# Layer 1 of a graph network: dense weights turned by transfers through memory, key one-hots in PSUM

## The reference

```
def _weighted_mean_agg(ft, w, src, dst, n_nodes):
    m = ft[src] * w[:, None]
    msum = segment_sum(m, dst, n_nodes)
    wsum = segment_sum(w, dst, n_nodes)
    safe = where(wsum > 0, wsum, 1.0)
    return where((wsum > 0)[:, None], msum / safe[:, None], 0.0)
neigh1 = _weighted_mean_agg(feat, w, src, dst, n)
neigh2 = _weighted_mean_agg(feat, w, dst, src, n)
```

## Time and profile before

| | us |
|---|---|
| median of 3 runs (9472.91 to 9473.69) | 9473.14 |
| the profiled execution | 9470.78 |
| its span, first to last instruction | 9469.0 |
| the stage of the change within it, first cell to last reversed product | 140.7 to 2975 |

### The profile page before, as it was taken

How to read it: one execution, slowest core, us unless ns; L and a number is a source line. 1 busy time by engine, 2 the same in 40 slices (tenths; PEclk the granted TensorE clock), 3 DMA queues, 4 the chain that set the end, 5 groups by cost and what they waited for, 6 DMA issues and landing times. The chain is left out here.

```text
span 9469.0 us, 228933 instructions
## 1 busy us (share of the span) xinstructions
PE 8637.6 (91%) x58595; PEld 6939.6 (73%) x58596; DVE 5874.3 (62%) x12349; ACT 5795.2 (61%) x15455; POOL 5415.5 (57%) x5229
## 2 busy tenths in 40 slices
PE   5999999999998899999988888888885899999998
PEld 5999999999997677775656666666654666666666
DVE  7777777787876677762125555555554555555555
ACT  5888888888885544440016677677763555555555
POOL 5777777777773000000005777777771677777775
PEclk7999999999999999999999999999998999999999
DMA  3111111111111122225544444444430222222222
GB/s 129 45 44 44 44 44 44 45 44 44 44 44 48 69 109 115 115 95 191 191 140 142 118 118 118 118 118 118 118 112 33 77 73 73 73 73 73 73 73 69
DMA packets 463488, 819.24 MB, mean 87 GB/s; under 512 B 160570, under 2 KB 330610, under 8 KB 443634
## 3 DMA queue, kind: packets, MB, share of 16 engines
q0 software_dynamic: 193536, 455.41, 16.6%
q1 hardware_dynamic: 269810, 362.04, 11.0%
HBM read 668.94 MB, written 147.98 MB: 86 GB/s over the span
## 5 line engine op out<-in xcount | busy, mean ns | idle before, releaser
L1776 POOL DMA_INDIRECT x<-table,p_gidx x1632 | 1542.4, 945 | 2375.3 <-ACT p_gidx L1813 1968.7
L618 POOL DMA_INDIRECT g_G<-table,g_runs x1776 | 2146.9, 1209 | 549.0 <-issue 538.8
L2228 POOL DMA_INDIRECT c_G<-table,c_gidx x1632 | 1543.7, 946 | 505.2 <-issue 497.0
L757 PE MATMUL g_ps_cell<-g_kw,g_loh 128*128 128x98 f32 x9472 | 1224.4, 273 | 28.6 <-DVE g_kw L675 28.6
L757 PEld LDWEIGHTS g_ps_cell<-g_kw,g_loh 128*128 128x128 f32 x9472 | 1154.6, 193 | 28.8 <-DVE g_kw L675 28.8
L1866 PE MATMUL p_ps_sum<-x 128*96 128x256 f32 x3264 | 898.5, 399 | 232.1 <-DVE hid L1802 223.1
L768 PE MATMUL g_ps_rev<-g_hrow,g_AT 128*128 128x129 f32 x7252 | 1047.6, 281 | 66.0 <-ACT g_AT L734 66.0
L768 PEld LDWEIGHTS g_ps_rev<-g_hrow,g_AT 128*128 128x128 f32 x7252 | 903.9, 192 | 94.0 <-ACT g_AT L734 94.0
L1866 PEld LDWEIGHTS p_ps_sum<-x 128*96 128x96 f32 x3264 | 469.0, 163 | 647.0 <-ACT x L1831 272.5
L1802 DVE TENSOR_TENSOR hid<-hid,p_ps_sum 96x256 f32 x1632 | 677.1, 415 | 363.8 <-DVE hid L1802 360.5
L1338 ACT CAST a_A<-a_ps_cell 128x392 bf16<-128x392 f32 x1184 | 510.8, 492 | 541.8 <-PE a_ps_cell L1372 541.8
(11 more groups left out here) (345 smaller groups left out, 16644.2 us busy)
## 6 DMA issues: line engine op xcount, KB each, us to landing
adj_save<-a_A SPq DMA_DIRECT2D x74, 1568.0 KB, 5.1
a_A<-adj_save SPq DMA_DIRECT2D x74, 1568.0 KB, 6.5
c_ed<-in_edge_dram SPq DMA_DIRECT2D x1632, 25.0 KB
g_G<-table,g_runs POOLq DMA_INDIRECT x1776
p_lhs<-in_edge_dram SPq DMA_DIRECT2D x1632, 16.0 KB
x<-table,p_gidx POOLq DMA_INDIRECT x1632
c_G<-table,c_gidx POOLq DMA_INDIRECT x1632
table<-m_rows SPq DMA_DIRECT2D x17, 384.0 KB
```

The costliest lines, as they stand in the source:

```text
L618: g.indirect_dma_start(G[:, e % GR, q, 0:D], None, table, bass.IndirectOffsetOnAxis(ap=runs[:, n % 2, 0, RQ * e + q:RQ * e + q + 1], axis= ...
L757: last = pe.matmul(ps_cell[q % 2][:, r * KEYS:(r + 1) * KEYS], loh[:, b, cell, :], kw[:, b, cell, :], start=True, stop=True)
L1776: g.indirect_dma_start(G[:, H * b + q, :], None, table2, bass.IndirectOffsetOnAxis(ap=gidx[:, b, q:q + 1], axis=0)).then_inc(gathered[b], 16)
L2228: g.indirect_dma_start(G[:, H * b + q, :], None, table, bass.IndirectOffsetOnAxis(ap=gidx[:, b, q:q + 1], axis=0)).then_inc(gathered[b], 16)
```

## The change

- **The dense matrix is no longer turned on TensorE.** Cells are made the other way round, with `kw` as weights and `loh` as the moving side, so that keys lie on partitions: 98 partitions by 4 x 128 columns a half. ScalarE copies a half into `X`, a ring of 8 halves. SyncE stores it to `turn_save` in memory (two batches), and after each four halves a quarter of a batch can be loaded back into `AT`, now with slots on partitions (32 partitions of 49 x 128 numbers a load). `AT` holds two whole batches.
- `turn`, the copies to `AT`, `ps_turn`, and the semaphores between them are gone. `backward` reads `AT` and waits for the four loads of its batch. It stands 5 halves later (`LATE`), at halves 6 to 15 of the next batch and 0 to 5 of the one after.
- **The key one-hots** are made in two operations of 4 slots, in float32, into the two freed PSUM banks, and `kw` is made from there in two operations as well. `number` is float32 now. `koh` has a wait for `oh_ready` of the chunk before.
- In the stage before this, the slots are numbered in another order, to fit the partitions of the loads.

The diff, cut to its core:

```
@@ stage_gru_sums
-                A = sb("g_A", [P, 2, KEYS, HALF], F32, ctx)
-                AT = sb("g_AT", [P, 2, TG * P], F32, ctx)
-                koh = sb("g_koh", [P, 2, 2, KEYS, CQ], BF16, ctx)
+                X = sb("g_X", [P, XR, CQ * P], F32, ctx)
+                AT = sb("g_AT", [P, 2, BUCKETS * P], F32, ctx)
-                ps_turn = [ps(f"g_ps_turn{k}", ctx) for k in range(2)]
+                ps_koh = [ps(f"g_ps_koh{k}", ctx) for k in range(2)]
@@ sync
+                        def store(n, bb, q):
+                            sp.wait_ge(evacd, HALVES * n + q + 3)
+                            sp.dma_start(turn_save[bb, CQ * q:CQ * (q + 1), :, :].rearrange("c k l -> k c l"),
+                                         X[0:KEYS, q % XR, :].rearrange("k (c l) -> k c l", c=CQ)).then_inc(stored[q // QT_HALVES], 16)
+                        def load_turned(m, b, z):
+                            sp.wait_ge(stored[z], 16 * QT_HALVES * (m + 1))
+                            sp.dma_start(AT[QSLOTS * z:QSLOTS * (z + 1), b, :],
+                                         turn_save[b, HALF // QUARTERS * z:HALF // QUARTERS * (z + 1), :, :].rearrange("c (j h) l -> (c j) (h l)", j=GRP)
+                                         ).then_inc(turned[b], 16)
+                        def body(i, bb):
...
+                            for q in range(HALVES):
+                                if known(n):
+                                    store(n, bb, q)
+                                if q == 1 and known(n - 1):
+                                    load_turned(n - 1, 1 - bb, QUARTERS - 1)
+                                if known(n) and q == 9:
+                                    if known(n - 2):
+                                        sp.wait_ge(rev_made, TGS * (n - 1))
+                                    load_turned(n, bb, 0)
+                                    load_turned(n, bb, 1)
+                                if known(n) and q == 13:
+                                    load_turned(n, bb, 2)
@@ vector, one_hots
-                            v.tensor_tensor(koh[:, b % 2, :, :, :],
-                                            key_tab[:, cells].rearrange("p (u r) -> p u r", u=2).unsqueeze(2).to_broadcast([P, 2, KEYS, CQ]),
-                                            number[:, :, :].unsqueeze(1).to_broadcast([P, 2, KEYS, CQ]), ALU.is_equal).then_inc(koh_made, 1)
+                            if not (isinstance(c, int) and c == 0):
+                                v.wait_ge(oh_ready, c)
+                            for u in range(2):
+                                half = bass.ds(c * CP + u * CQ, CQ)
+                                v.tensor_tensor(ps_koh[u][:, 0:CQ * KEYS].rearrange("p (r k) -> p r k", r=CQ),
+                                                key_tab[:, half].unsqueeze(2).to_broadcast([P, CQ, KEYS]),
+                                                number[:, :].unsqueeze(1).to_broadcast([P, CQ, KEYS]), ALU.is_equal).then_inc(koh_made, 1)
...
+                            for u in range(2):
+                                half = bass.ds(c * CP + u * CQ, CQ)
+                                v.wait_ge(koh_made, 2 * c + u + 1)
+                                last = v.tensor_tensor(kw[:, b % NOH0, u * CQ:(u + 1) * CQ, :],
+                                                       ps_koh[u][:, 0:CQ * KEYS].rearrange("p (r k) -> p r k", r=CQ),
+                                                       w_tab[:, half].unsqueeze(2).to_broadcast([P, CQ, KEYS]), ALU.mult)
+                            last.then_inc(oh_ready, 1)
@@ scalar
+                                    if q % QT_HALVES == 0:
+                                        z = q // QT_HALVES
+                                        if z >= 2:
+                                            s.wait_ge(stored[z - 2], 16 * QT_HALVES * (n + 1))
+                                        elif known(n - 1):
+                                            s.wait_ge(stored[z + 2], 16 * QT_HALVES * n)
...
+                                    s.copy(X[0:KEYS, q % XR, :], ps_cell[q % 2][0:KEYS, :]).then_inc(evacd, 1)
@@ tensor
-                                last = pe.matmul(ps_cell[q % 2][:, r * KEYS:(r + 1) * KEYS], loh[:, b, cell, :], kw[:, b, cell, :], start=True, stop=True)
+                                last = pe.matmul(ps_cell[q % 2][0:KEYS, r * P:(r + 1) * P], kw[:, b, cell, :], loh[:, b, cell, :], start=True, stop=True)
...
-                            pe.wait_ge(at_ready, g + 3)
                             pe.wait_ge(rev_added, g + 1)
                             if k == 0:
+                                pe.wait_ge(turned[b], 16 * QUARTERS * (i + 1))
                                 pe.wait_ge(gathered[b], 16 * (i + 1))
```

More of the change, by code:

```diff
@@ L57 @@
 TG = 3
+LATE = 5
+XR = 8
+QT_HALVES = 4
+QUARTERS = HALVES // QT_HALVES
+QSLOTS = P // QUARTERS
 RQ = 4
@@ L382, in _ @@
                         for j in range(GRP):
-                            last = v.tensor_scalar(slots[:, :, j, :], base[:, 0, :].rearrange("g (h c) -> g h c", h=2), float(j), None, ALU.add)
+                            last = v.tensor_scalar(slots[:, :, :, j], base[:, 0, :].rearrange("g (h c) -> g h c", h=2), float(j), None, ALU.add)
                         then(last)
@@ L571, in stage_gru_sums @@
                 consts, koh_made, oh_ready, built, evacd = (sem(f"g_{k}") for k in ("consts", "koh_made", "oh_ready", "built", "evacd"))
-                turned, at_ready, rev_made, rev_added, applied = (sem(f"g_{k}") for k in ("turned", "at_ready", "rev_made", "rev_added", "applied"))
+                rev_made, rev_added = sem("g_rev_made"), sem("g_rev_added")
+                stored = [sem(f"g_stored{z}") for z in range(QUARTERS)]
+                turned = [sem(f"g_turned{b}") for b in range(2)]
                 away, weighted, run_made, added = (sem(f"g_{k}") for k in ("away", "weighted", "run_made", "added"))
@@ L596, in _, with load_runs @@
                     def _(sp):
-                        def load(i, bb):
-                            n = 2 * i + bb
+                        def load_runs(n, bb):
                             if not (isinstance(n, int) and n < 2):
```

57 lines of the change are left out of this document (17 added, 40 removed).

## The result

The kernel after takes **10561.05 us** (median of 6, 10547.39 to 10567.44) against 9472.52 for the kernel before beside it (9470.49 to 9473.69): ratio **1.1147, 95% interval 1.1133 to 1.1162**. It is slower by 1089 us, and the prediction was wrong in sign and size. The profiled execution has a span of 10565.7 us against 9469.0.

A forecast was written before the change was run, and what follows sets the result against it. TensorE was taken to bound the 37.97 us batch; afterwards VectorE's 34.6 x 1.03 gives 35.6. Over 74 batches that saves 175 us, plus 10 in the tail: 9287 us, chance 0.50; 8-in-10 range 9195 to 9450.

The forecast's parts named there:

- TensorE 31.4: TensorE's time a batch: 36.85 us less 5.4 for the transposes; passes stay at 0.11 us.
- VectorE 34.2: VectorE's work a batch: 30.0 us before, plus 4.2 for the split key one-hot operations.
- rival 3: PSUM operands hold VectorE up: 39.1 us a batch, 84 us slower, 9547 us; chance 0.09.
- a chunk costs 0.52 us more: VectorE's `koh` and `kw` as two operations each: 0.46 + 0.06 us more a chunk, 4.2 us a batch.
- GpSimd 34.1 to 36.9: GpSimd's time a batch: 31.1 us plus gather delays, `kw` no longer delaying; 37.8 before.
- rival 1: GpSimd is the bound, `koh` and `loh` still delaying gathers: batch 36.9 us, 9384 us; chance 0.20, shared with half-price PSUM.
- SyncE issues 21 transfers of some 0.5 us: SyncE's issuing a batch, followed by the claim that the last quarter's load is covered: 9 us against some 5.
- Gathers have slack too: GpSimd's gathers: the ring lets them run up to three runs, half a batch, ahead.
- DMA 24.2 us a batch: DMA engines two thirds full: stores 176, loads 120 and gathers 91 engine us, 387 / 16.
- The tail: End of the stage: 31 us before; 7 us of transfers plus 17 products at 0.8 make 21, 10 less.
- should mostly go: VectorE's own waits, as TensorE runs ahead; 0.4 us a batch of "issue" ahead of `fwd` kept.
- rival 4: DMA is the bound: slow loads, uneven shares or stores queued behind loads; batch 38.4 us, 9504 us; chance 0.09.

The follow-up runs named there:

- e4: Kernel after with the `runs` load issued a batch earlier, key one-hots made by one operation over both PSUM banks and `kw` by one: 9390.74 us, ratio 0.9913.
- e16: e4 with six increments of an unused semaphore per chunk in VectorE's loop: ratio 0.9961 to the kernel before, in a set where every kernel ran slower.
- e5: Kernel before with six increments of an unused semaphore per chunk in VectorE's loop: 9563.61 us, ratio 1.0098.
- e6: Kernel after with only the `runs` load moved, issued behind the first store of the batch before: 9767.21 us, ratio 1.0311.

## Why the prediction was wrong, step by step

**TensorE 31.4, right as work.** Transposes and their waits are gone, and the cells, turned round, still go at 0.11 us a pass: four of them start 0.88 us apart (4031.01 to 4031.89) and six loads of reversed tiles 0.66 (4031.89 to 4032.55) in the late part of the stage:

```profile
4031.01 0.93 PEld L799 LDWEIGHTS g_ps_cell<-g_loh,g_kw 128*98 128x98 f32 x8
4031.89 0.75 PEld L810 LDWEIGHTS g_ps_rev<-g_hrow,g_AT 128*128 128x128 f32 x6
4032.55 0.93 PEld L799 LDWEIGHTS g_ps_cell<-g_loh,g_kw 128*98 128x98 f32 x8
```

But the engine did not run at full clock any more: 0.86 in the stretch, and right after its idle 8.99 us eight passes of a run take 2.10 us (above), about twice the time of these, 8.65 us later:

```profile
1420.84 1.06 PE L821 MATMUL g_ps_run<-g_Gw,g_roh 128*128 128x130 f32 x8
```

The granted clock is 0.50 from 1412.19 to 1416 us, the lower of its two levels (1.2 GHz), and 1.00 from 1420 us. A stall costs again after it has ended, and no term had that.

**VectorE 34.2, right as durations; its loop was never looked at.** `ps_koh` pairs take (1075.22 - 1074.27) = 0.95 us, as forecast, and `kw` the same. PSUM costs nothing here, so rival 3 falls. Missing was what the length of the loop costs: two more operations and two more waits in every chunk, and each turn begins with 6.8 us in which VectorE stands while instructions are fetched. That is 3.4 to 4.4 us a batch, 3.9 by the distances of the loads. The step "a chunk costs 0.52 us more" counted elements and starts, not the length of the loop. The holes come and go with the length (e4, e16); that the fetch itself is what VectorE waits for is argued from the packets, and e5 shows that a fetch need not cost so much.

**GpSimd 34.1 to 36.9, right in its mechanism.** The gather that meets a `kw` is no longer held by it:

```profile
1470.53 1.31 POOL L659 DMA_INDIRECT g_G<-table,g_runs  x1 [0.30 <-issue]
...
1470.94 1.03 DVE L722 TENSOR_TENSOR g_kw<-g_ps_koh,w_tab 128x392 f32<-128x392 f32 x2
```

The `loh` before it ended at 1471.02 and the gather 0.82 us after that (1471.84), in the middle of the two `kw` operations. The mean of a gather fell from 1193 ns to 229.5 / 223 = 1.03 us; it is 1092 ns in e4, 25 x (1.09 + 0.30) = 34.8 us a batch, within the range. The sign that was named for rival 1, ScalarE waiting for gathered rows, did appear (97.1 us), but not for its reason: GpSimd stood idle for 174.6 us.

**SyncE: here the prediction failed.** It says "SyncE issues 21 transfers of some 0.5 us", asks only whether the last quarter's load is covered, and puts the gathers at no cost: "Gathers have slack too". The first two hold: the issues are short, and TensorE has no wait for that load among its rows. The third doesn't, since the gathers wait for `g_runs` 19.4 us a batch. Not asked was what stands behind the stores. The sixteen stores each wait for a cell copy, so that the queue, which in the kernel before held only the loads of `runs` and stood at the wait for a free buffer, a batch ahead of need, now runs in step with ScalarE. The `g_runs` load of a batch is asked for only behind the last store of the batch before. The row that would have told it was in the trace of before (1000 to 1500 us):

```profile
SPq L601 <- ACT g_Gw L715: 481.5, 13, 37.2
```

SyncE spends its time there waiting for the buffer to come free, and the load starts at once when it does. What the trace of before could have said, for every queue that gets new work: what else is issued from it, and how long ahead. Price: 15 us less what the holes take, 11 us a batch; 794 us by e6.

**DMA 24.2 us a batch: mis-sized.** Stores and loads were 176 + 120 = 296 engine us by the rows of another stage; e4 shows 432, and its DMA share is 0.90 x 36.8 = 33.1 us a batch. The mistake did not decide in the kernel after, where the engines are at 0.66. It may be a part of why e4 stands at 36.8 and not at 35.6; ScalarE's waits there for gathered rows are 20.0 us in 500 and those ahead of `g_X` for stores 0.9 us, so that the rows put at most 1.5 us a batch on it.

**The tail, right in the price of a group, wrong in the sum.** Two groups of products in it, 12 passes each row:

```profile
4062.58 1.42 PEld L810 LDWEIGHTS g_ps_rev<-g_hrow,g_AT 128*128 128x128 f32 x12 [0.17 <-DVE x L687]
4064.17 1.42 PEld L810 LDWEIGHTS g_ps_rev<-g_hrow,g_AT 128*128 128x128 f32 x12 [0.17 <-DVE x L687]
```

1.59 us for two groups is 0.8 each, as forecast. But the tail as a whole, from the last cell to the last reversed product, was 2974.9 - 2942.4 = 32.5 us before and is 4070.7 - 4038.4 = 32.3 in the kernel after, and 28.9 in e4, not 10 us less. The starts of the last passes (first and last start in each row) and TensorE's timeline at the end:

```profile
L757 PE MATMUL g_ps_cell<-g_kw,g_loh x9472: 247/275/533, 140.7 to 2942.4; 128*128 128x98 f32 x198
L799 PE MATMUL g_ps_cell<-g_loh,g_kw x9472: 270/273/532, 141.7 to 4038.4; 128*98 128x128 f32 x198
L810 PE MATMUL g_ps_rev<-g_hrow,g_AT x7252: 272/276/584, 204.3 to 4070.7; 128*128 128x129 f32 x196
...
4055.47 15.54 PE L810 MATMUL g_ps_rev<-g_hrow,g_AT 128*128 128x129 f32 x98 [6.51 <-issue]
```

The 98 passes are the 17 groups of the last batch, behind 6.5 us for its last load. Ahead of both stand seven groups of the batch before, since products now come five halves later; the forecast had left these out.

**The sum.** With both faults mended, e4, 9390.74 us stands against the forecast of 9287: 82 us gained where 186 had been forecast. The gap of 104 us is 1.2 us a batch (36.80 against 35.6), 89 us, and some 15 beside, of which the tail is 6. The 1.2 us a batch lie in VectorE's waits, which "should mostly go". It is busy 450.48 us in 13.6 batches, 33.1 a batch, which is the 34.2 of the forecast less the 1.1 for two operations saved. Its waits are 3.5 a batch (23.6 us for reversed products, 19.2 by "issue" ahead of `fwd`, 5.0 for cells, in 500 us), where the forecast had 0.4 and 3%. So the work was rightly priced and what stands between the engines was not. None of the four rivals was a late load, so the range could not hold it: the nearest, rival 4, spoke of "stores queued behind loads on the one queue of SyncE", the same queue in the other direction.

## What to carry to other kernels

When transfers that wait for work are put on a queue, list everything that is issued from it and ask for each how far ahead of its use it was issued before and is now; an early load placed behind a late store is late, and moving one line here was worth 794 us. Count instructions in a loop too, not only their time: an operation split in two can cost little itself and yet make the loop long enough to be fetched again at each turn, which shows as packets on the instruction queue and, in most kernels here, as one unexplained hole per turn. If the busy shares of all engines fall together, look for a ring of waits, not for a bound.

## What the runs showed that was not expected

- A hole of 6.8 us per turn on VectorE in the kernel after, 7.7 at most in e6 and 5.6 in e16, with 26 to 32 packets of fetched instructions in 500 us against 2 or 3; in e5, with 34 packets, only waits of under 2 us.
- One operation may write both PSUM banks (784 elements in two pieces of 392), in 981 ns; two operations of 392 take 572 each and start 0.48 us apart.
- TensorE's granted clock was 0.86 in the kernel after, where it waits up to 14.5 us at a time, 0.95 in e6 (up to 5.8), and 1.00 in e4 (up to 2.0). Right after a wait of 8.99 us the clock was 0.50, the lower of its two levels (1.2 GHz), and the passes took twice their time.
- A load into 64 partitions in place of two into 32 did not change the time (0.985 against 0.9854), with the DMA engines busy 0.68 to 0.72.
